# Copying y out of PSUM on ScalarE instead of VectorE in a gated linear-attention layer

## The reference, cut to what matters

```
u = layernorm(x)
q, k, v = u Wq^T, u Wk^T, u Wv^T ;  a = sigmoid(u Wg^T)       # 16 heads of 64
h_t = a_t * h_{t-1} + k_t v_t^T ;  y_t = q_t h_t               # per head, over tokens
x = x + layernorm(y) Wo^T
g, p = layernorm(x) w_gate^T, layernorm(x) w_up^T              # int weights / 127
x = x + (silu(g) * p) w_down^T
```

## Time and profile before

| | |
|---|---|
| median of 3 runs | 1476.25 us (1475.36 to 1478.11) |
| the profiled execution | 1479.63 us |
| its span, core 5, the slowest | 1478.1 us (cores 1462.9 to 1478.1) |
| granted clock, share of full, by core | 0.811 to 0.826 |
| PE busy | 948.1 us, 64% |
| DVE busy | 513.5 us, 35% |
| ACT busy | 330.7 us, 22% |
| the 64 copies L731 on DVE | 44.1 us busy, 688 ns each |
| pair loops of groups 0 to 3, from about | 281.6, 432.0, 589.1, 743.1 |

### The profile page before, as it was taken

The page is one execution under the profiler, slowest core; times in us unless marked ns, Lnnn a source line. Parts: engine busy times, 40 slices in busy tenths (PEclk is TensorE's granted clock), DMA queues, the critical chain, the costliest instruction groups (busy, mean ns, idle before and its releaser), DMA issues.

```text
span 1478.1 us, 17760 instructions; the slowest of 8 cores (1462.9 to 1478.1 us)
## 1 busy us (share of the span) xinstructions
PE 948.1 (64%) x5892; PEld 448.5 (30%) x5892; DVE 513.5 (35%) x928; ACT 330.7 (22%) x691; POOL 136.0 (9%) x193
## 2 busy tenths in 40 slices
PE   0024275766765687656754000079999999999997
PEld 0002232332233232432332000034444444444443
DVE  0022325456645664457566344012112212211110
ACT  0031622533163316322122122011111111100000
POOL 2000000010101010110011001011101101100110
PEclk9967677777976777568876555589999999999999
DMA  9903120121323130311012356944344344312322
GB/s 144 175 4 97 41 60 0 30 74 57 100 30 60 64 106 8 66 65 57 8 44 82 93 125 141 171 44 43 31 42 41 36 40 43 44 46 97 114 86 100
DMA packets 144456, 99.97 MB, mean 68 GB/s; under 512 B 123504, under 2 KB 123504, under 8 KB 144368
## 3 DMA queue, kind: packets, MB, share of 16 engines
q0 software_dynamic: 72816, 81.02, 27.3%
q1 hardware_dynamic: 71552, 17.83, 6.6%
HBM read 93.86 MB, written 16.78 MB: 75 GB/s over the span
## 4 chain that ended last, share of the span: by engine, by line
PE 51%; DVE 19%; DMA 11%; ACT 6%; issue 5%; another core or an unknown queue 5%; SPq 2%; DVEq 1%; ACTq 0%; POOL 0%; POOLq 0%
PE p_g L910 11%; PE p_d L949 11%; PE p_u L923 11%; PE p_fr L339 5%; DMA s_x2T<-s_a 4%; DVE s_nL L360 3%; DMA s_wd<-wdi 3%; DVE s_nL L435 3%; PE p_pp L575 2%; DVE s_ht L667 2%; PE p_py L475 2%; DVE s_y L731 2%; DMA s_xlnT<-s_xln 2%; PE p_py L406 2%
## 5 line engine op out<-in xcount | busy, mean ns | idle before, releaser
L910 PE MATMUL p_g<-s_x2T,s_wgu 128*128 128x512 bf16 x768 | 183.1, 382 | 152.4 <-DMA s_wgu<-wui 152.4
L923 PE MATMUL p_u<-s_x2T,s_wgu 128*128 128x512 bf16 x768 | 181.6, 379 | 0.0
L929 DVE SCALAR_TENSOR_TENSOR s_hff<-p_u,s_act 128x512 bf16<-128x512 f32 x96 | 66.4, 692 | 294.5 <-PE p_u L923 262.2
L949 PE MATMUL p_d<-s_wd,s_hff 128*128 128x512 bf16 x768 | 165.9, 379 | 1.2 <-DVE s_hff L929 1.2
L910 PEld LDWEIGHTS p_g<-s_x2T,s_wgu 128*128 128x128 bf16 x768 | 75.4, 98 | 244.1 <-issue 154.5
L339 PE MATMUL p_fr<-s_xlnT,s_wg 128*128 128x512 bf16 (+1 forms) x320 | 83.0, 426 | 66.5 <-DMA s_xlnT<-s_xln 64.7
L916 ACT ACTIVATE s_act<-p_g 128x512 f32<-128x512 f32 x96 | 57.3, 597 | 270.2 <-PE p_g L910 270.2
L949 PEld LDWEIGHTS p_d<-s_wd,s_hff 128*128 128x128 bf16 x768 | 75.1, 98 | 92.0 <-issue 1.7
L923 PEld LDWEIGHTS p_u<-s_x2T,s_wgu 128*128 128x128 bf16 x768 | 75.2, 98 | 91.0 <-issue 0.8
L575 PE MATMUL p_pp<-s_wo,s_E 128*128 128x512 bf16 x256 | 77.3, 470 | 24.5 <-DVE s_xr L600 24.5
L705 PE MATMUL p_py<-s_V,s_P 64*64 64x64 bf16 x256 | 29.9, 237 | 90.0 <-DVE s_P L641 90.0
(11 more groups left out here) (109 smaller groups left out, 1127.4 us busy)
## 6 DMA issues: line engine op xcount, KB each, us to landing
s_x<-x2d POOLq DMA_DIRECT2D x32, 512.0 KB, 4.9
s_x<-xs POOLq DMA_DIRECT2D x18, 512.0 KB, 8.9
s_xr<-xs POOLq DMA_DIRECT2D x16, 512.0 KB, 4.3
x2d<-s_xr POOLq DMA_DIRECT2D x16, 512.0 KB, 2.9
out<-s_x POOLq DMA_DIRECT2D x16, 512.0 KB, 3.0
s_wd<-wdi POOLq DMA_DIRECT2D x1, 6144.0 KB, 45.1
s_wgu<-wgi POOLq DMA_DIRECT2D x24, 256.0 KB, 5.2
s_wgu<-wui POOLq DMA_DIRECT2D x24, 256.0 KB, 5.8
```

The lines of the kernel that those rows point to most:

```text
L910: addD("t", lambda t, buf=buf, t4=t4, j=j, pb=pb: t.matmul(p_g[pb][:], s_wgu[buf][:, TILE * j:TILE * (j + 1)], s_x2T[:, 2048 * j + 512 * t ...
L923: addD("t", lambda t, buf=buf, t4=t4, j=j, pb=pb: t.matmul(p_u[pb][:], s_wgu[buf][:, 1024 + TILE * j:1024 + TILE * (j + 1)], s_x2T[:, 2048 ...
L929: addD("v", lambda v, hc=hc, t4=t4, pb=pb: v.scalar_tensor_tensor(s_hff[:, 2048 * hc + 512 * t4:2048 * hc + 512 * (t4 + 1)], p_u[pb][:], S ...
L949: addD("t", lambda t, ts=ts, buf=buf, hf=hf, hcc=hcc: t.matmul(p_d[buf][:, 512 * hf:512 * (hf + 1)], s_hff[:, 2048 * hcc + TILE * ts:2048 ...
```

## The change

The four copies of y out of PSUM are made by ACT, as `activation` with `AF.Copy`, and no longer by DVE. They keep their place in the program's text, so they now stand in ACT's list. The semaphores follow: PE's product into `p_py` and the transpose of `s_y` wait for SE in place of VE. The copies' wait for ACT's earlier statistics of the same half of `s_y` falls away, since both now run on one engine.

```diff
                 if bk < 4:
-                    return [(VE, pyf[bk - 2])]
+                    return [(SE, pyf[bk - 2])]
...
-                        wait=([(VE, max(FR["qk_done"], pyf[par]))]
+                        wait=([(VE, FR["qk_done"]), (SE, pyf[par])]
                               if h == 0 else ()),
...
-                        O.add("v", lambda v, ysl=ysl, par2=par2, hp=hp:
-                              v.tensor_copy(
+                        O.add("s", lambda s, ysl=ysl, par2=par2, hp=hp:
+                              s.activation(
                             s_y[64 * par2:64 * (par2 + 1),
...
                                 "p (q two o) -> p q two o", two=2, o=C)[:, :, hp, :],
                             p_py[64 * hp:64 * (hp + 1),
                                  512 * par2:512 * (par2 + 1)].rearrange(
-                                "p (q o) -> p q o", o=C)),
+                                "p (q o) -> p q o", o=C),
+                            AF.Copy),
                             wait=(([(TE, TE.n),
-                                    (YT, G["yt_slot"].get(w % 2, 0)),
-                                    (SE, G["yst_slot"].get(w % 2, 0))])
+                                    (YT, G["yt_slot"].get(w % 2, 0))])
                                   if (par2 == 0 and hp == 0) else ()),
-                            inc=VE)
-                    pyf[par2] = VE.n
+                            inc=SE)
+                    pyf[par2] = SE.n
...
-                    wait=[(VE, VE.n)])
+                    wait=[(SE, SE.n)])
```

## The result

The changed kernel takes 1534.25 us (median of 10 runs) against 1478.81 for the kernel before beside it: ratio 1.0386, 95% interval 1.0363 to 1.0410, so about 57 us slower. Two of the ten executions on each side were in a slower state of the chip, 7 to 9% longer; the ratios leave such executions out, and without them the medians here are 1533.90 and 1477.18 us. Its profiled execution took 1534.18 us.

A forecast was written before the change was run, and what follows sets the result against it. PE and DVE bound the pair loops, handing work to each other, with ACT loose. Terms 72.9 + 1.8 - 3.9 - 6.8 = +64.0 us, on the median 1476.25, gave 1540.3 us, range 1527 to 1555.

The forecast's parts named there:

- What bounds the kernel, and what the tiles wait for: Pair loops: PE and DVE alternate; ACT's next-group layer-norm tiles, 26.0 us, cost nothing before but would wait behind pair 0's copies.
- The queue of ACT: ACT's strictly first-in, first-out queue holds ready layer-norm tiles behind waiting copies; a 25.79 us wait was read as showing it.
- the first rival: In ACT's queue, layer-norm tiles pass pair 0's copies or are not held: -10.1 us, 1466.2 us; chance 0.05.
- Term 1: Groups 0 to 2, first y copy to gate matmuls: transposes go out 24.3 us later in each, +72.9 us.
- What I named as late next: Pair 0's y statistics and pair 1's copies end 7.8 us after the tiles, just short of the transposes' 8.5.
- Term 2: Pair 2 of groups 0 to 2: copies delay ACT's first Exp of the gate matmuls by 0.6 us, +1.8 us.
- Term 3: End of the pair loops of groups 0 to 2: scans start sooner, gain 1.3 us each, -3.9 us.
- Term 4: Last group, without layer-norm tiles: pair 0 to 1 gains 3.2 us, then 1.2 three times, -6.8 us.
- Dear copies: Copies on ACT take 1.33 us a piece: +20 us over all groups, 1560 us; chance 0.07.
- Late transposes: Groups 0 to 2: transposes wait for another DMA transfer, +4.3 us three times, 1553 us; chance 0.05.

The follow-up runs named there:

- only the wait: Kernel before, copies on DVE, with each layer-norm tile of the next group also waiting for the y matmuls of pair 0: 1540.10 us, ratio 1.0424.
- half the tiles: Changed kernel with two of the four layer-norm tiles written ahead of pair 0's copies: 1497.29 us, ratio 1.0138 against the kernel before.
- the whole front ahead: Changed kernel with four layer-norm tiles and the s_xlnT transposes written ahead of pair 0's copies: 1453.77 us, ratio 0.9858 against the kernel before.

## Why the prediction was right

It said 1540.3 us (1527 to 1555), slower, and the cause. Measured were 1534.25, or 57 us more than before where the sum said 64. The step that makes the loss was right and its size nearly so; the smaller terms were right in part, and one had the wrong sign.

**What bounds the kernel, and what the tiles wait for.** Right, and shown from both sides: the wait without the copies costs 4.2%, the copies without the wait gain 0.6%.

**The queue of ACT.** That the tiles stay behind the copies is shown. That it is the queue which holds back a ready instruction is not, and the earlier trace rows do not show it, as I had read them. L258 was not ready at 400.0. In this program each instruction of ACT waits by the semaphore SE for the one before it, L258 too (its line in the lists of the change names SX, ST, VE and SE). And L258 writes the right half of s_nL (columns 1024 to 2047), which L443 and L446, just ahead of it, still had to read. With that wait in the program the tiles stand behind the copies whatever the queue does. So the first rival was excluded by the program's own waits, more firmly than its chance of 0.05 says. No run here leaves the wait on SE out, so none tells the two apart.

**Term 1.** The step was right, the size 3.7 too large: of the 72.9 predicted 69.2 were measured. By the means of 8 cores and three groups, the transposes went out 4.6 us after the first copy and now go out at 28.6, a shift of 24.0 for 24.3. The copies took 2.64 us in place of 2.76, the tiles 25.7 (294.66 to 320.35) in place of 26.0. That is 0.9 us of the 3.7. Most of the rest is a part that I had taken as fixed: from issue of the transposes to the first gate matmul it was 8.4 us and is now 7.5. What shortens it I did not test; it is 7.4 in the run with only the wait and 7.5 in the one with half the tiles. What I named as late next, the statistics and the copies of pair 1, held nothing: on the cores with complete rows PE starts before these copies end. DVE's earlier finish ahead of pair 1 was swallowed, as said: PE's wait at L339 grew by some 26 us (27.45 on core 5, 0.63 to 1.55 before), more than the 24 by which the transposes came later.

**Term 2.** Wrong in sign on the whole, -1.2 for +1.8. The slip of ACT's first Exp is there in group 1 of core 0:

```profile
527.76 2.64 ACT L731 ACTIVATE s_y<-p_py 64x512 bf16<-64x512 f32 x4 [8.37 <-PE p_py L715]
530.49 0.60 ACT L345 ACTIVATE s_nL<-p_fr 128x512 f32<-128x512 f32 x1
...
532.06 3.61 PE L339 MATMUL p_fr<-s_xlnT,s_wg 128*128 128x512 bf16 x16 [0.40 <-ACT s_S L349]
```

Exp starts 2.73 us after the first of the copies, 2.13 before, and PE waits 0.40 us for the bank, less than the 0.6 I priced. But I had priced all loops by one in which Exp came early. In the kernel before it started 2.1 to 2.4 us after the first copy in 8 of 24 loops (8 cores, three groups) and 3.0 to 3.4 us after it in the other 16, where copies that end at 2.64 hold nothing.

That the stretch as a whole became shorter is not due to the copies: with them on DVE the experiment with only the wait has 69.8 us here in the mean of 8 cores, the changed kernel 69.7, the kernel before 70.9. It goes with the granted clock. Two of these stretches in the kernel before, core 2, groups 0 and 1 (columns as in the earlier trace rows, the clock is the third number from the end):

```profile
326.99:349.40 22.41, 14.70 (x177) 8.04 (x176) 12.67 (x19) 9.10 (x20) 3.15 (x4) 0.80 0.19 65
477.41:501.74 24.33, 16.15 (x177) 8.39 (x176) 12.68 (x18) 9.10 (x20) 3.03 (x4) 0.78 0.17 59
```

In the kernel before 6 of the 24 stretches take 22.4 to 22.95 us, all at 0.80, and the other 18 take 23.5 to 24.4 us at 0.74 to 0.79. In the changed kernel 16 take 22.9 to 23.1 us at 0.80, and 8 take 23.6 to 24.0 us at 0.78 or 0.79. At the same clock the two kernels agree. So the change in this stretch is in how many loops were granted the higher share; what sets that, no run here shows.

**Term 3.** -2.9 for -3.9. The scans start 9.6 to 10.7 us after the first copy of y(3), 10.0 in the mean, against 10.9 to 11.2 before. L575 sets that, as said; it ends 4.3 to 5.4 us after that copy, and the row I used, 4.4 us, was one of the short ones.

**Term 4.** -6.1 for -6.8. Pair 0 to 1 gained more (3.7 for 3.2), the others not alike: 0.8, 0.3 and, behind the copies of the last pair, 1.3, for 1.2 each. The limit was L575, as said, but I had taken it to start and to last as before. In the earlier trace rows it starts 0.74 us ahead of the copies of pair 1; in the changed kernel, core 5, it starts 0.28 ahead of them (817.82 and 818.10), so the end that DVE waits for came later than I had it. In the two pairs behind it also lasts longer. Kernel before, then changed kernel, core 5, pairs 2 and 3:

```profile
782.55 4.78 PE L575 MATMUL p_pp<-s_wo,s_E 128*128 128x512 bf16 x16
799.49 4.84 PE L575 MATMUL p_pp<-s_wo,s_E 128*128 128x512 bf16 x16
...
833.94 5.35 PE L575 MATMUL p_pp<-s_wo,s_E 128*128 128x512 bf16 x16
850.54 5.58 PE L575 MATMUL p_pp<-s_wo,s_E 128*128 128x512 bf16 x16
```

The granted clock was 0.75 in the first two and 0.67 and 0.64 in the last two. So the epilogue, which began 5.56 us after the first copy of each pair before, begins 4.9, 5.3 and 5.6 us after it now: part of what DVE gave back, PE took at a lower clock. The 1.3 us at the end lie in the last L575, which I had not looked at: 6.14 us at 0.59 before, 5.25 us at 0.68 now.

**The rest.** The first stretch came out 1.6 us shorter and the last 0.7, where the change does nothing. Together with the terms this makes the 56.4 of the mean span. One pair of cores says little here: core 5 went from 1478.1 to 1524.0, core 0 from 1469.6 to 1532.6. The forecast of the absolute time also used 1476.25 as its base, 0.9 below the later one of 1477.18 us.

**The rivals.** That the tiles get past the copies fell with the profile after: in each loop they start behind the four copies. Dear copies fell with 591 ns. Late transposes fell: they were quicker, 7.5 us from issue to the gate matmuls in the mean against 8.4 before.

## What to carry to other kernels

Moving an instruction to an idle engine moves its wait as well, and everything written behind it on that engine then waits too, here because the program has each instruction of ACT wait for the one before it, if for nothing else. Before you move one, look at what that engine does during its idle time in front of the new place, for here its idleness was the result of having run ahead. When work must be moved so, write the run-ahead work in front of it; here that turned 3.9% of loss into 0.6% of gain, and with the transposes moved as well into 1.4%.

## What the runs showed of the hardware

A copy of 64x512 fp32 out of PSUM to bf16 takes 591 ns on ACT and 688 on DVE, and four in a row 2.64 against 3.06 us. Four transposes of s_xln queued right behind those of s_ktm delayed the latter by no more than 0.3 us. With the whole front ahead, core 2, the second transpose of s_ktm in each group (L530) lands 3.7, 4.7 and 5.5 us after its issue (least, median and most of five), and 3.6, 4.6 and 5.2 us before. The first one (L524), which the first chunks need, takes at most 3.7 us in both and has landed by the time those of s_xln are issued.

The same 16 matmuls of L575 on core 5 took 4.8 us at a granted clock of 0.75, 5.35 us at 0.67, 5.58 us at 0.64 and 6.14 us at 0.59. So part of what shorter waits gave back in the last loop went to a lower clock; what lowers it, no run here shows.
